# Two layers of cross-attention: the last unit's first blocks turned in squares, late keys summed a step behind their load, ScalarE scaling the last unit's other blocks

## What is computed

```python
def _cross_attention(q_in, kv_in, wq, bq, wk, bk, wv, bv, wo, bo, bias_k, bias_v):
    qh = (q_in @ wq + bq).reshape(b, q_len, H, K)
    kh = (kv_in @ wk + bk).reshape(b, t, H, K)
    vh = (kv_in @ wv + bv).reshape(b, t, H, K)
    kh = jnp.concatenate([kh, jnp.broadcast_to(bias_k, (b, 1, H, K))], axis=1)
    vh = jnp.concatenate([vh, jnp.broadcast_to(bias_v, (b, 1, H, K))], axis=1)
    logits = jnp.einsum('bqhk,bthk->bhqt', qh, kh) / jnp.sqrt(K)
    weights = jax.nn.softmax(logits, axis=-1)
    ctx = jnp.einsum('bhqt,bthk->bqhk', weights, vh).reshape(b, q_len, H * K)
    return ctx @ wo + bo
```

## Time and profile before

| | us |
|---|---|
| median of three runs | 1750.84 |
| the profiled execution | 1745.42 |
| its span | 1743.6 |
| TensorE busy | 1721.1 |
| VectorE busy | 1190.7 |
| ScalarE busy | 752.0 |
| GpSimd busy | 872.1 |

### The profile page before, as it was taken

The page is one execution under the profiler, slowest core; times in us unless marked ns, Lnnn a source line. Parts: engine busy times, 40 slices in busy tenths (PEclk is TensorE's granted clock), DMA queues, the critical chain, the costliest instruction groups (busy, mean ns, idle before and its releaser), DMA issues.

```text
span 1743.6 us, 30234 instructions
## 1 busy us (share of the span) xinstructions
PE 1721.1 (99%) x10854; PEld 1674.9 (96%) x10854; DVE 1190.7 (68%) x2718; ACT 752.0 (43%) x1624; POOL 872.1 (50%) x727
## 2 busy tenths in 40 slices
PE   8999999999998999999999999999999999999999
PEld 4899999999998999999999999999999999999999
DVE  3667676666877766667876666668766666677675
ACT  3634334334553333335453344345533333454654
POOL 2684252455583453534873523555834535336754
PEclk9999999999999999999999999999999999999999
DMA  7732332223452322324342323234423223204432
GB/s 278 253 117 79 89 89 51 71 84 97 138 157 64 81 83 70 90 50 142 115 126 74 86 49 76 83 106 131 145 57 83 63 75 86 79 19 142 132 128 80
DMA packets 162784, 175.09 MB, mean 100 GB/s; under 512 B 99660, under 2 KB 115276, under 8 KB 162636
## 3 DMA queue, kind: packets, MB, share of 16 engines
q1 hardware_dynamic: 159388, 168.86, 33.2%
q10 hardware_dynamic: 3248, 4.30, 0.7%
HBM read 150.67 MB, written 5.14 MB: 89 GB/s over the span
## 4 chain that ended last, share of the span: by engine, by line
PE 92%; DVE 5%; ACT 1%; DMA 1%; issue 1%; SPq 1%; ACTq 0%; DVEq 0%
PE psum L819 29%; PE psum L820 29%; PE psum L821 29%; PE psum L1157 2%; PE psum L853 2%; DVE key_stage_late L1710 1%; DMA key_stage_late<-head_w_dram 1%; DVE prob L1989 1%; DVE pT L1684 1%; DVE centred L1890 0%; SPq L563 0%; PE psum L832 0%; DVE a_lo L1684 0%; PE psum L828 0%; ACT prob L1520 0%
## 5 line engine op out<-in xcount | busy, mean ns | idle before, releaser
L653 POOL TENSOR_TENSOR wbuf_hi<-stage,zero_col 128x512 fp32r<-128x512 f32 x256 | 273.1, 1067 | 667.5 <-PE psum L821 503.4
L708 POOL TENSOR_TENSOR wbuf_lo<-stage,wbuf_hi 128x512 fp32r<-128x512 f32 x256 | 337.5, 1318 | 20.1
L819 PE MATMUL psum<-pT,ctx_rows_hi 128*128 128x250 f32 (+1 forms) x1152 | 330.4, 287 | 6.7 <-DVE pT L1684 6.5
L820 PE MATMUL psum<-pT,ctx_rows_hi 128*128 128x250 f32 (+1 forms) x1152 | 330.2, 287 | 0.0
L821 PE MATMUL psum<-pT,ctx_rows_lo 128*128 128x250 f32 (+1 forms) x1152 | 329.6, 286 | 0.0
L819 PE MATMUL psum<-ctxT_hi,a_hi 128*125 128x362 f32 (+1 forms) x832 | 277.1, 333 | 0.5
L821 PE MATMUL psum<-ctxT_hi,a_lo 128*125 128x362 f32 (+1 forms) x832 | 273.0, 328 | 0.0
L820 PE MATMUL psum<-ctxT_lo,a_hi 128*125 128x362 f32 (+1 forms) x832 | 273.0, 328 | 0.0
L819 PE MATMUL psum<-a_hi,wbuf_hi 128*128 128x400 f32 x720 | 253.3, 352 | 0.9 <-DVE xT L1905 0.9
L820 PE MATMUL psum<-a_lo,wbuf_hi 128*128 128x400 f32 x720 | 247.6, 344 | 0.0
L821 PE MATMUL psum<-a_hi,wbuf_lo 128*128 128x400 f32 x720 | 247.5, 344 | 0.0
(11 more groups left out here) (220 smaller groups left out, 3384.8 us busy)
## 6 DMA issues: line engine op xcount, KB each, us to landing
stage<-head_w_dram SPq DMA_DIRECT2D x256, 256.0 KB, 2.9
mlp_stage<-mlp_w_dram SPq DMA_DIRECT2D x32, 512.0 KB, 3.3
ctx_rows_in<-ctx_dram SPq DMA_DIRECT2D x20, 768.0 KB, 4.5
ctxT_in<-ctxT_dram SPq DMA_DIRECT2D x20, 724.0 KB, 4.8
p_b<-p_scratch SPq DMA_DIRECT2D x64, 200.0 KB, 3.5
sorted<-prob SPq DMA_DIRECT2D x256, 48.0 KB, 2.0
key_stage<-head_w_dram SPq DMA_DIRECT2D x22, 256.0 KB, 5.1
pT<-prob SPq DMA_DIRECT2D x96, 48.0 KB, 2.0
```

Source lines behind the costliest of these rows:

```text
L653: return nc.gpsimd.tensor_tensor(out, in_, zero_col[0:in_.shape[0], :].broadcast_to(tuple(in_.shape)), ALU.add)
L708: nc.gpsimd.tensor_tensor(lo, held, hi.bitcast(F32), ALU.subtract).then_inc(stage_free, 1)
L819: pe.matmul(out, a_h, x_hi, start=start, stop=False)
L820: pe.matmul(out, a_h, x_lo, start=False, stop=False)
```

## The change

Four things are changed.

1. `in_squares` now also holds for block 0 of the last unit in batches 1, 2 and 3. These blocks are no longer turned by TensorE but by VectorE and SP's queue. Their sorts all stand ahead of the load of piece 59 (`o12`).
2. The reloads of context columns and rows of batches 0, 1 and 2 move from behind the loop over the pieces to behind the sorts of (5,1,0), (5,2,0) and (5,3,0).
3. There are four late keys in each of phases 0 and 1 instead of five: summed at (0,1), (0,3), (1,1) and (1,3), loaded behind piece 9 and behind the sorts of (0,2,0), (1,0,0) and (1,2,0). So 24 keys are made before the layers, and the sums among the last residuals are 5, 1, 1, 2 instead of 5, 0, 0, 2.
4. The nine blocks of the last unit that TensorE still turns are scaled by ScalarE (`scale_probs`, a copy with a scale column, in place) and no longer by VectorE; VectorE still makes the reciprocal. `turn_probs` waits for ScalarE's `a_norm` there.

```diff
--- before.py
+++ after.py
@@ -89,9 +89,9 @@
 
 KEYS = 7
 LATE_KEYS_IN = 2
-LATE_KEYS_AT = [(0, 1), (0, 2), (0, 3), (1, 2), (1, 3)]
+LATE_KEYS_AT = [(0, 1), (0, 3), (1, 1), (1, 3)]
 FIRST_LATE_KEY_BEHIND = 9
-LATE_KEYS_BEHIND_SORTED = [(0, 2, 0), (0, 3, 0), (1, 0, 0), (1, 3, 0)]
+LATE_KEYS_BEHIND_SORTED = [(0, 2, 0), (1, 0, 0), (1, 2, 0)]
 KEYS_BEFORE = LAYERS * H - LATE_KEYS_IN * len(LATE_KEYS_AT)
 
 
@@ -120,10 +120,16 @@
 
 
 def in_squares(k, b, x):
-    return 0 < k + (x == 0) and k < len(UNITS) - 1 and not (k in LATE and b < 2) and not (x == 1 and b in (0, NB - 1))
+    return 0 < k + (x == 0) and (k < len(UNITS) - 1 or x == 0 < b) and not (k in LATE and b < 2) and not (x == 1 and b in (0, NB - 1))
 
 
 HELD = 2
+def scaled_by_act(k, b, x):
+    return k == len(UNITS) - 1 and not in_squares(k, b, x)
+
+
+BY_ACT = [at for at in SCORED if scaled_by_act(*at)]
+A_LAYER = len(BY_ACT)
 BY_PE = [at for at in TURNED if not in_squares(*at)]
 PE_AT = {at: i for i, at in enumerate(BY_PE)}
 PE_LAYER = len(BY_PE)
@@ -346,7 +352,7 @@
         dv_s, p0_add, p0_kept = sems("dv_s p0_add p0_kept")
         p0_out = [sem(f"p0_out{j}") for j in range(ROW_BUFS)]
         p0_ld = [sem(f"p0_ld{j}") for j in range(P0_BUFS)]
-        masked_s, prob_set, squares_turned = sems("masked_s prob_set squares_turned")
+        masked_s, prob_set, squares_turned, a_norm = sems("masked_s prob_set squares_turned a_norm")
         sorted_ld = [sem(f"sorted_ld{j}") for j in range(HELD)]
         p0_sent = [sem(f"p0_sent{j}") for j in range(HELD)]
         y_mm, y_hi, y_done = sems("y_mm y_hi y_done")
@@ -383,6 +389,10 @@
 
         def by_chunk(ap):
             return ap.rearrange("p (t i g) -> p t i g", g=GROUPS, i=SQUARE)
+
+        def scaled_before(ph, i):
+
+            return ph * (S_LAYER - A_LAYER) + sum(not scaled_by_act(*at) for at in SCORED[:i + 1])
 
         def sorted_blocks(ph, at):
 
@@ -593,6 +603,9 @@
                             while reads and T_AT[LAST_BLOCK_OF[reads[0]]] < T_AT[at]:
                                 load_first_probs(ph, reads.pop(0))
                             sort_squares(ph, *at)
+                            if not last and at[0] == LAST_UNIT and at[1] > 0:
+                                reload_ctx_columns(ph, at[1] - 1)
+                                reload_ctx_rows(ph, at[1] - 1)
                             if ph < LATE_KEYS_IN and at in LATE_KEYS_BEHIND_SORTED:
                                 load_late_key_weights(next(keys))
                     for h in reads:
@@ -605,9 +618,6 @@
                         sp.wait_ge(x_st, ph * 16 + 16)
                         sp.dma_start(x_held[:, :, :], x_d[1 - half]).then_inc(hn_ld, 16)
                 if not last:
-                    for b in range(NB - 1):
-                        reload_ctx_columns(ph, b)
-                        reload_ctx_rows(ph, b)
                     reload_ctx_columns(ph, NB - 1)
                 load_weights(ph, W_AT["v", H - 1])
                 for h in range(H - 4, H - 1):
@@ -1146,7 +1156,10 @@
                         return
                     i = S_AT[k, b, x]
                     rows = BLOCKS[UNITS[k][x]][1]
-                    pe.wait_ge(s_norm, ph * S_LAYER + i + 1)
+                    if scaled_by_act(k, b, x):
+                        pe.wait_ge(a_norm, ph * A_LAYER + BY_ACT.index((k, b, x)) + 1)
+                    else:
+                        pe.wait_ge(s_norm, scaled_before(ph, i))
                     turn = PE_AT[k, b, x]
                     if turn == 0:
                         pe.wait_ge(s0_row, ph + 1)
@@ -1519,6 +1532,15 @@
                         out, scored = by_chunk(out), by_token(scored)
                     nc.scalar.activation(out, scored, ACT.Exp, bias=st[:, 0:1], accum_out=st[:, 2:3]).then_inc(s_exp, 1)
 
+                def scale_probs(k, b, x):
+                    if not scaled_by_act(k, b, x):
+                        return
+                    i = S_AT[k, b, x]
+                    rows = BLOCKS[UNITS[k][x]][1]
+                    act.wait_ge(s_rcp, ph * S_LAYER + i + 1)
+                    nc.scalar.activation(prob[0:rows, i % 2, :], prob[0:rows, i % 2, :], ACT.Copy,
+                                         scale=stats[0:rows, i % 2, 3:4]).then_inc(a_norm, 1)
+
                 def probs_hi(k, b, x):
                     rows = BLOCKS[UNITS[k][x]][1]
                     wait(act, u_mm, ph * U_LAYER + U_AT[k, b])
@@ -1591,6 +1613,7 @@
                         exps(k, b, 0)
                         if before is not None:
                             send_first_row(*last)
+                        scale_probs(k, b, 0)
                         run_pieces((k, b, "a"))
                         if (k, b) == VARIANCE_IN:
                             hidden_roots(ph)
@@ -1600,6 +1623,7 @@
                         if (k, b) == (0, 1) and ph > 0:
                             ctx_rows_hi(ph + TURNS - 1, NB - 1)
                         exps(k, b, 1)
+                        scale_probs(k, b, 1)
                         if before is not None:
                             attended_hi(*before)
                         probs_hi(k, b, 0)
@@ -1609,6 +1633,7 @@
                             probs_hi(k, b, 1)
                             exps(k, b, 2)
                             send_first_row(k, b, 1)
+                            scale_probs(k, b, 2)
                         if (k, b) == STEPS[-2] and reload:
                             ctx_columns_hi(ph + TURNS, 0)
                     before = k, b
@@ -1845,7 +1870,7 @@
                 some_key_sums(3)
                 turned_lo(7)
                 for m in range(DC):
-                    some_key_sums((5, 0, 0, 2)[m])
+                    some_key_sums((5, 1, 1, 2)[m])
                     residual(1, m)
 
             def norm_centre(j, x, n):
@@ -1985,11 +2010,13 @@
                     st = stats[0:rows, i % 2, :]
                     dve.wait_ge(s_exp, ph * S_LAYER + i + 1)
                     nc.vector.reciprocal(st[:, 3:4], st[:, 2:3]).then_inc(s_rcp, 1)
+                    if scaled_by_act(k, b, x):
+                        return
                     dve.wait_ge(s_rcp, ph * S_LAYER + i + 1)
                     nc.vector.tensor_scalar(prob[0:rows, i % 2, :], prob[0:rows, i % 2, :], st[:, 3:4], None, ALU.mult)\
                         .then_inc(s_norm, 1)
                     if in_squares(k, b, x):
-                        dve.wait_ge(s_norm, ph * S_LAYER + i + 1)
+                        dve.wait_ge(s_norm, scaled_before(ph, i))
                         nc.vector.transpose(prob[:, i % 2, :], prob[:, i % 2, :]).then_inc(squares_turned, 1)
 
                 def probs_lo(k, b, x):
```

## The result

The changed kernel takes 1751.82 us (median of 20 executions) where the kernel before took 1749.38 us: a ratio of 1.0019, 95% interval 1.0012 to 1.0025. It is slower by 2.4 us by the medians and 3.3 us by the ratio, where 2.8 us faster was forecast; the time itself lies inside the stated range of 1741.0 to 1753.0 us. The profiled execution took 1752.57 us, its span is 1750.8 us.

A forecast was written before the change was run, and what follows sets the result against it. TensorE was taken to bound the kernel, busy 1721.1 of 1743.6 us. Late keys -6.2, added keys +0.5 and the last unit +2.9 sum to -2.8 us from 1750.84: 1748.0 us, range 1741.0 to 1753.0 us.

The forecast's parts named there:

- Late keys: Phases 0 and 1: TensorE's stalls behind VectorE's late key sums shrink, -6.2 us, bounds 4.5 to 7.5 us gained.
- The second rival: Sums at (0,3) and (1,1) meet GpSimd, 3 us of the 6.2 come back: about 1750.8 us; chance 0.15.
- Single head: Before the layers: two more keys delay the last residual, which TensorE needs for the mean; +0.5 us, from 0 to 1.5.
- Work off TensorE: Last unit: 12 sets of three transposes leave TensorE at 0.32 us a set, 3.9 us of work removed.
- the lower bound: Last unit: -5.8 us, if 3.9 us of work and 1.9 us of TensorE's waits all go.
- The last unit: TensorE's saving is waited for again, and more: +0.9 us in each of phases 0 to 2, +0.2 in phase 3, +2.9 us together.
- parts 1 and 3: The prediction's own parts: 1 is transposes taken off TensorE, 3 is ScalarE scaling the last unit; together +2.9 us.
- the upper bound of 7: Last unit: +7 us at most for squares and ScalarE's scaling together, at 2.3 us a phase.
- ScalarE's place: Last unit: scaling takes 0.60 us on ScalarE; in (5,1) it stands before `attended_hi`, which starts 2.3 us later.
- third rival: Squares of (5,3,0) land late and ScalarE waits; 5 us more, 1753 us, or 1755 us with GpSimd's lock; chance 0.13.
- The slower side: The whole kernel slower by more than 0.2% (3.5 us): chance 0.13.

The follow-up runs named there:

- the fastest kernel: The kernel after with VectorE scaling the last unit and the last piece of `hidden_scale` in (5,3) behind `normalise` of block 2: 1738.13 us, ratio 0.9939.
- its repeat: The changed kernel, unchanged, measured once more beside the kernel before: 1751.98 us against 1749.33 us, ratio 1.0019.
- the two experiments that keep both squares and nine ScalarE scalings a phase: The changed kernel with GpSimd waiting for the maximum of (5,3,2), 1745.79 us; and with `hidden_scale`'s last piece in (5,3) behind `normalise` of block 2, 1746.49 us.

## Why the prediction was wrong

- **Late keys, -6.2 us with bounds of -4.5 to -7.5: right.** -5.7 and -6.9 us by the marks in the two traces of after, -6.4 us in the kernel with late keys alone. The second rival (their gain lost beside GpSimd) falls: the pieces of the sums at (0,3) took 0.28 to 0.29 us, those at (1,1) 0.82 us for the first of four and 0.28 us for the others. (Its price adds up to 1751.0 us, not 1750.8.) TensorE has no wait at (1,1), as costed, and 0.35 us at (0,3) of phase 1; 0.4 us at (1,3) of phase 1 was not in the sum.
- **Single head, +0.5 us: right.** It is +0.1 to +0.6 us in six of the seven traces of changed kernels at full clock there, and +1.6 us in the seventh, which had 0.8 us of it at 50 us already. That an execution may lose 2 to 3 us there to the clock was not in the prediction, which took a clock of 1.0 for granted from one execution.
- **Work off TensorE, -3.9 us: the count is right, and how much of it arrives stays open.** 324 transposes for 360. In the fastest kernel the four last transposes of the phases have gained 4.3 us in sum against late keys alone, counted from (5,0,2) as below, of the 5.8 us of work and waits that the lower bound had; at the end of the program it is 1.7 us between these two traces, and 3.5 to 5 us by the ratios.
- **The last unit, +2.9 us for parts 1 and 3 together: this step failed.** It is +8.9 and +10.7 us, of which 1.5 and 3.3 us are half clock; without that 7.4 and 7.3 us, past the upper bound of 7. By transposes in after, with the lead at (5,0,2) taken out: block 2 of (5,1) is 0.1 us early in phase 0 (+0.2 forecast), that of (5,2) 0.5 us late (+0.2 to +0.4), that of (5,3) 2.0, 2.0 and 2.5 us late in phases 0 to 2 (+0.9). Phase 3, with no GpSimd beside it and no reload, is 1.2 us late (+0.2). That is ScalarE's scaling: without squares it is 1.1 us late there, and with squares and VectorE scaling 0.5 us early.
- **The term that was mis-sized is the low part of (5,3,0).** I gave `p_row`'s copy back as a saving and let the low part stay as it was. But it changed its operand: with squares both its inputs are in SBUF. It takes 1.32 us there instead of 0.54, and `hidden_scale` behind it 1.34 instead of 0.88. That is +1.24 us in the chain, three times, 3.7 us of the 4.5 us that the step is off; phase 3 has another 1.0 us. The trace of before had this price. Its groups by form:

```profile
L1684 DVE TENSOR_TENSOR pT<-psum,pT 128x375 fp32r<-128x375 f32 x104 | 56.5, 543 | 9.5 <-ACT pT L1287 8.9
L1684 DVE TENSOR_TENSOR pT<-sorted,pT 128x384 fp32r<-128x384 f32 x64 | 39.1, 611 | 11.1 <-ACT pT L1287 11.0
```

  The mean from `sorted` is 0.07 us above that from PSUM: a mean over many undisturbed ones and four at 1.1 to 1.6 us. I read neither row. I had named the lock for the multiply that leaves, and not for the instruction that comes under it.
- **ScalarE's place.** The scaling took 0.62 us (0.60 assumed). Its second effect was argued away in (5,3): it stands in front of `attended_hi`, so `a_hi` starts at 461.55 (459.39 in before), and what VectorE has behind it moves against GpSimd's instructions: the low part starts just behind the start of one, and not near its end as with VectorE scaling.
- **Squares late (third rival): no.** ScalarE never waited for them in (5,3). The slower side came from the mechanism that I had counted as speaking for the change.
- **The end.** From the last product to the end after takes 4.62 us, and before 3.69 us. I had nothing for it (last section).

The Trainium skill, "SBUF — State Buffer", Who interferes with whom, has the rule for the mis-sized term: a VectorE instruction with two inputs in SBUF contends with a GpSimd instruction that reads SBUF, and one with a single SBUF input does not, outside the faster modes. The runs agree: 1.32 us from `sorted` beside GpSimd, 0.55 us with GpSimd held back, 0.54 us from PSUM beside GpSimd. They also show that the price depends on the moment: 0.60 us from `sorted` where GpSimd's instruction was nearly over. The added transpose, with one SBUF input, stayed at 0.58 us.

## What to carry to other kernels

When an edit moves an operand from PSUM to SBUF, cost every reader again, beside what GpSimd does at that moment; a mean over the whole kernel hides the price. Two edits that are each harmless alone can meet in one chain: price them together, in the step where TensorE already waits, and look there for an instruction that nobody needs yet and that can go behind the chain (here `hidden_scale`: 4 to 5.5 us for one line with squares, and nothing without them). And take the clock of several executions before taking it for constant.

## What was not expected of the hardware

**Some waits of TensorE have a slower clock at their end.** Half of the waits of 2.61 to 2.65 us have, 3.4 us at 1.2 GHz, and one of 1.95 us, but not those of 1.72 and 2.01 us in before and none of the twelve of 1.16 to 1.66 us; the numbers stand under The clock. In the single head the half clock came without any gap ahead of it, for 3.4 or 6.8 us, in 6 of the 14 traces of this study. What decides it stays open.

**The end is 0.94 us longer in four traces.** From the start of the last product to the end of the span, after, its repeat and the two experiments that keep both squares and nine ScalarE scalings a phase take 4.62 to 4.65 us; the other ten traces have 3.67 to 3.69 us. DMA queues during the last 7 us, after and then before (packets, MB, share):

```profile
q1 hardware_dynamic: 576, 0.82, 32.2%
q14 instruction: 1, 0.01, 0.3%
```

```profile
q1 hardware_dynamic: 576, 0.82, 31.9%
```

In after one packet of the instruction queue falls among the last stores, 1.8 us ahead of the end of the span. It does so in the other three traces with the longer end, and in none of the ten with the shorter one. That the end waits for it fits, but was not tried.
